# Attention stage: which tile splits a late piece of the input, and where the DMA queue waits for all splits

## The reference

```
qkv = x @ w_qkv.T                       # 16 heads of 32
q, k = [q*cos, q*sin], [k*cos, k*sin]   # angle = theta * position
per chunk of 128 tokens:
  scores = (q @ k.T) * diag_decay
  o      = scores @ v + (q*q_decay) @ state
  state  = block_decay*state + (k*k_decay).T @ v
x = layernorm(x + o @ w_proj.T)
```

## Time and profile before

| | |
|---|---|
| median of 3 runs | 1555.37 us (1551.93 to 1556.06) |
| the profiled execution | 1554.85 us |
| its span, first to last instruction | 1553.0 us |
| PE busy | 1402.9 us, 90% |
| DVE, POOL, ACT busy | 900.2, 763.5, 661.8 us |
| mean granted PE clock | 0.956 |
| attention stage | about 0 to 296 us of the span |

### The profile page before, as it was taken

How to read it: one execution, slowest core, us unless ns; L and a number is a source line. 1 busy time by engine, 2 the same in 40 slices (tenths; PEclk the granted TensorE clock), 3 DMA queues, 4 the chain that set the end, 5 groups by cost and what they waited for, 6 DMA issues and landing times.

```text
span 1553.0 us, 31650 instructions
## 1 busy us (share of the span) xinstructions
PE 1402.9 (90%) x10327; PEld 770.8 (50%) x10328; DVE 900.2 (58%) x1826; ACT 661.8 (43%) x1250; POOL 763.5 (49%) x691
## 2 busy tenths in 40 slices
PE   5999999799999999999886469999999999999990
PEld 2554555444444444445443226666666666666650
DVE  7765566677757576636988864444444444444435
ACT  7322222455444545423445434444444444444443
POOL 4555454510101101333645356766767677777755
PEclk9999999899999999999998579999999999999995
DMA  8776976698796969522312636888988998776866
GB/s 274 150 136 129 192 150 119 156 318 298 233 287 231 297 223 298 183 72 82 84 23 95 227 100 122 179 184 176 196 193 176 205 190 194 138 113 90 178 81 228
DMA packets 213453, 271.73 MB, mean 175 GB/s; under 512 B 133993, under 2 KB 135561, under 8 KB 212368
## 3 DMA queue, kind: packets, MB, share of 16 engines
q1 hardware_dynamic: 177776, 211.40, 46.8%
q0 software_dynamic: 35616, 59.58, 23.8%
HBM read 158.92 MB, written 101.71 MB: 168 GB/s over the span
## 4 chain that ended last, share of the span: by engine, by line
PE 77%; DVE 13%; DMA 3%; issue 2%; ACT 2%; POOL 2%; SPq 0%; DVEq 0%; ACTq 0%; POOLq 0%
PE bank L888 20%; PE bank L909 11%; PE bank L721 7%; PE bank L715 6%; PE bank L738 6%; PE bank L593 6%; PE bank L601 5%; PE bank L879 5%; PE bank L668 2%; DMA ARENA<-ARENA 2%; PE bank L898 2%; DVE ARENA L1253 1%; PE bank L632 1%; PE bank L633 1%; PE bank L660 1%
## 5 line engine op out<-in xcount | busy, mean ns | idle before, releaser
L888 PE MATMUL bank<-ARENA,XT 128*128 x1908 | 364.7, 327 | 2.1 <-issue 1.5
L1804 POOL DMA_INDIRECT accs<-X,WA x159 | 252.8, 1590 | 99.9 <-issue 39.4
L888 PEld LDWEIGHTS bank<-ARENA,XT 128*128 128x128 f16 x1908 | 180.5, 98 | 125.3 <-issue 9.4
L1343 DVE COPY XT<-bank 128x1024 f16<-128x1024 f16 x159 | 110.0, 692 | 186.0 <-PE bank L879 158.4
L1797 POOL DMA_INDIRECT XT<-x_rows,WA x159 | 166.6, 1048 | 86.9 <-issue 43.6
L909 PE MATMUL bank<-ARENA,XT 128*128 x795 | 197.4, 379 | 1.1 <-issue 1.0
L1382 ACT ACTIVATE ARENA<-ARENA 128x512 f16<-128x512 f32 (+2 forms) x128 | 89.3, 708 | 224.1 <-DVE ARENA L1101 132.0
L1622 ACT ACTIVATE XT<-bank 128x192 f32<-128x192 f32 x159 | 52.5, 330 | 287.8 <-PE bank L888 249.7
L593 PE MATMUL bank<-XT,STG 128*128 128x512 f16 x640 | 151.5, 384 | 7.4 <-DVE ARENA L1147 7.3
L1650 POOL TENSOR_TENSOR rstd<-mv,mhalf 128x1 f32<-128x1 f32 x28 | 5.7, 202 | 280.0 <-DVE mv L958 280.0
L601 PE MATMUL bank<-WA,XT 128*128 128x512 f16 x540 | 124.7, 380 | 1.9 <-DVE ARENA L1044 1.9
(11 more groups left out here) (244 smaller groups left out, 2173.6 us busy)
## 6 DMA issues: line engine op xcount, KB each, us to landing
w_scratch<-WA SPq DMA_DIRECT2D x64, 640.0 KB, 3.9
ARENA<-w_scratch SPq DMA_DIRECT2D x64, 640.0 KB
ARENA<-w_exp SPq DMA_DIRECT2D x48, 640.0 KB, 5.3
WA<-w_exp SPq DMA_DIRECT2D x16, 640.0 KB, 5.1
ARENA<-ARENA SPq DMA_DIRECT2D x32, 256.0 KB, 4.1
accs<-ARENA SPq DMA_DIRECT2D x20, 256.0 KB, 3.2
X<-x SPq DMA_DIRECT2D x4, 1024.0 KB, 5.6
ARENA<-wc SPq DMA_DIRECT2D x8, 512.0 KB, 6.1
```

The lines of the kernel that those rows point to most:

```text
L888: mm = pe.matmul(d, xTb[k.u % 2][:, a * KD + kd, :], weights(sl, b, kd * 2 * DFF, 2 * DFF), start=(a, b, kd) == (0, 0, 0), stop=(a, b, kd) ...
L1343: dve.tensor_copy(xTb[k.u % 2].rearrange("p c n -> p (c n)"), bank[k.u % 2][:, :].bitcast(F16)).then_inc(xt_sb, 1)
L1804: pool.indirect_dma_start(accs, bass.IndirectOffsetOnAxis(blkout[:, i:i + 1], 0), yD[i % 8], None, compute_op=ALU.add).then_inc(y_out[i % ...
```

## The change

Which late piece is handled in which tile is now a table: pieces 10 and 11 in tile 1, 12 in tile 2, none in tile 3, 13 to 15 in tiles 4 to 6 as before. PE's wait for all eight splits goes from before tile 7 to before tile 11, with a wait for six before tile 7, and its loop of tiles 7 to 14 becomes two. SP's wait for all eight splits goes from behind load_x(2) and load_x(3) to ahead of each of the int8 loads, that is from after turn(7) to after turn(9).

```diff
         LATE = 10
+        late = {1: (10, 11), 2: (12,), 4: (13,), 5: (14,), 6: (15,)}
...
                 elif n < 9:
                     load_x(n - 5)
+                elif n < 12:
                     sp.wait_ge(x_split, len(x_pieces))
-                elif n < 12:
                     sp.dma_start(*raws[n - 9]).then_inc(b_raw, 16)
...
             with pe.Fori(TB - 1, 2 * TB - 1) as t:
                 attention(t, False, False)
+            pe.wait_ge(x_split, 6)
+            with pe.Fori(2 * TB - 1, 3 * TB - 1) as t:
+                attention(t, False, False)
             pe.wait_ge(x_split, len(x_pieces))
-            with pe.Fori(2 * TB - 1, NT - 1) as t:
+            with pe.Fori(3 * TB - 1, NT - 1) as t:
                 attention(t, False, False)
...
-                if isinstance(t, int) and 1 <= t <= NPA - LATE:
-                    hi_piece(LATE + t - 1)
+                if isinstance(t, int):
+                    for n in late.get(t, ()):
+                        hi_piece(n)
...
-                if isinstance(t, int) and 1 <= t <= NPA - LATE:
-                    split_piece(LATE + t - 1)
+                if isinstance(t, int):
+                    for n in late.get(t, ()):
+                        split_piece(n)
```

## The result

The changed kernel takes 1543.56 us (median of 4 runs, 1542.99 to 1544.77) against 1555.7 for the kernel before beside it: a ratio of 0.9929, interval 0.9915 to 0.9944. The forecast was 1544.0.

A forecast was written before the change was run, and what follows sets the result against it. PE, busy 1402.9 us or 90% of the span, was taken as the bound. Terms -4.70 - 9.16 + 1.81 + 1.2 = -10.85 us took 1554.85 to 1544.0 us; range 1539.0 to 1550.0.

The forecast's parts named there:

- The gap before tile 7: First layer's attention: with both waits moved, PE's idling before tile 7 and its scores goes, clock stays up: -9.16 us.
- Rival 2: Tile 7: the load of a quarter of x delays the transposes, scores still wait; 6.7 us won, 1548.1; chance 0.15.
- The second hold in tile 1: POOL's second split holds DVE's third angle step, lengthening PE's gap before L1044 to 3.1 us: +1.81 us, bounds 0 to 3.6.
- The gap before tile 3: With piece 11 split in tile 1, PE's wait before tile 3 and the slower matmuls behind it go: -4.70 us.
- The loop cut in two: PE's loop of tiles 7 to 14: one more entry into fresh code shows nothing uncovered: 0, at most some tenths.
- The sum: Whole kernel: -4.70 - 9.16 + 1.81 + 1.2 = -10.85 us, from 1554.85 to 1544.0.
- the clock (1.2): Tile 2: PE's clock falls around the 3.1 us gap, slowing matmuls: +1.2 us, bounds 0 and 1.7.
- Rival 1: Tile 1: the second split is free, DVE's third angle step goes ahead of POOL, gap stays 1.31; 1541.0 us; chance 0.15.
- Rival 3: Across the kernel: most is given back by fresh loop code, clock falls elsewhere and the port; about 1552 us; chance 0.07.
- Rival 4: Tiles 1 and 2: ACT waits for piece 11 or 12 not yet landed, PE stops too; slower; chance 0.03.

## Why the prediction was right, point by point

- **The gap before tile 7, -9.16.** Measured -9.16 (31.30 against 40.46), with both waits gone, no long wait of SP for POOL and no idle PE before the scores. Rival 2, with the 1 MB load, falls: the q transpose of tile 7, issued 5.5 us behind the load, took 4.2 us and the k transpose 6.3. The prediction took both waits away together and did not say which one costs more; putting each back alone shows it (SP's +9.9, PE's +5.3 in tiles 7 and 8).
- **The second hold in tile 1, +1.81.** Measured +1.82, with two steps of 2.51 and 2.52 us and the gap of PE at 3.12 (3.1 said). None, one, two and three splits gave 0, 1, 2 and 3 held DVE instructions, so the exclusion is shown.
- **The gap before tile 3, -4.70.** Measured -4.06. No wait of L669 for POOL is left, but tile 3 is 16.29: PE waits 0.47 us for the k transpose, which takes 7.68 us instead of 6.18, and that is most of the 0.64 us by which the tile is long. This was missed. I had compared the start of the transposes with PE's arrival only at their usual 6.18.
- **The loop cut in two, 0.** Missed, with small and opposite pieces: +0.21 in tile 11, -1.47 in the last tile. The row I rested it on (the start of out_proj in the last tile) shows that PE does not wait for its code; it does not show what fetching the code does to the transposes.
- **The sum, -10.85.** The next layer begins exactly 10.85 us earlier. That it agrees to the last digit is luck: tile 3, tile 5, tile 1 and the first mark lose 2.4 us against the sum, tile 11 and the way to the next layer 0.3, and the clock (1.2) and the last tile (1.5) give it back.
- **Rival 1** (13.9 us less) was wrong for the change, but describes the kernel with one split in each tile: 12.9 us less by its ratio. **Rival 3** wanted 6.2 us or more given back; tiles 1, 3, 5 and 11, the first mark and the way to the next layer gave back 2.7. **Rival 4**: no wait of ACT's L1383 for a load is in the trace.

Two things stay open. Tile 1 is 16.4 to 16.7 us in all eleven edited kernels' profiles and 15.87 in that of before. In two of them (the changed kernel's and that with one split in each tile) the first mark stands at 38.83 us and half clock reaches 2.2 to 2.4 us into the tile, and PE is busy 0.8 to 0.9 us longer by it (16.49 and 16.59 us against 15.68), the whole difference; in the nine others the mark stands at 37.1 to 37.7 and PE waits 0.87 to 1.10 us for ACT before out_proj. Why the first mark moves was not tried. And the two measurements of the changed kernel, -11.0 and -7.2 us by their ratios, differ by more than the stretches of the attention stage do; I can only say that the part behind it scatters that much.

## What to carry to other kernels

When two engines wait for the same event, look for the one whose queue holds transfers that others need: here that wait cost 9.9 us and the other 5.3, and moving the other alone gained nothing. A helper's work that is pulled forward into a quiet engine can still stop its neighbour, so ask what the other engine runs in those microseconds, and place it where that engine reads PSUM or idles; here both pieces in tile 0 instead of tile 1 were worth a further 3.3 us in tile 2. (The whole stage is 4.3 us shorter, 242.33 against 246.62, but the rest is small differences that this edit was not meant to make, such as the long transpose of tile 5, which comes and goes.) Write a clock loss behind a gap of this length down as two cases, not as one number.

## What the hardware showed that I had not expected

**Instruction fetches go with stretched DMA transposes.** The instruction queue q8 moves packets of some 16 KB over the same DMA engines. From tile 3 on, the twelve profiles hold 29 transposes that took 5.9 to 6.1 us instead of 4.2 (q) or 7.4 to 7.7 instead of 6.2 (k), and in each of the 29 a q8 packet was under way. Not each packet makes one: several fell beside a transpose that kept its time, and several beside one of 4.4 to 5.2 us. In the changed kernel (two places of the chain of waits, and the instruction queue's row from 86 to 87 us):

```profile
81.07 7.68 DMA ARENA<-ARENA
...
107.34 5.88 DMA ARENA<-ARENA
```

```profile
q8 instruction: 1, 0.02, 7.4%
```

A long transpose costs 0.2 to 0.8 us where PE has work to run beside it (tiles 3 to 6 and 11) and 1.3 to 1.9 us where it has none (last tile: 17.59 and 17.63 us with a long k transpose, 15.7 to 16.3 without). In tile 3, at the entry to a new loop, it comes in every profile without a gap there; the one in tile 5 comes in tile 4, 5, 6 or 7 or not at all. That the packet is the cause is argued from this coincidence; adding loops added packets and one long transpose, which supports it but does not prove it.

**The same length of gap can cost the clock or not.** Idle for 3.11 to 3.12 us, three of six profiles kept 2.4 GHz. In the three others the clock fell 0.6 us before PE's gap ended, 0.04 us behind its end, or 0.9 us behind it. With 3.50 and 3.74 us in tiles 3 and 7 each of the five such gaps lost 1.3 to 1.7 us, and with 1.30 us none lost anything. But 3.50 us is no border either: before the first matmul of the feed-forward layer PE idles 3.4 to 3.8 us in each of the twelve profiles, and in two of them (the waits alone, the pieces alone) the clock stays at 2.4 GHz. PE's timeline there, first of the changed kernel, then of the one with the waits alone:

```profile
285.45 2.29 PE L719 MATMUL bank<-XT,WA 128*128 128x512 f16 x8 [3.78 <-issue]
287.54 3.21 PE L725 MATMUL bank<-XT,ARENA 128*128 128x512 f16 x8
```

```profile
286.26 1.89 PE L719 MATMUL bank<-XT,WA 128*128 128x512 f16 x8 [3.78 <-issue]
287.98 1.89 PE L725 MATMUL bank<-XT,ARENA 128*128 128x512 f16 x8
```

The gap is 3.78 us in both; the sixteen matmuls behind it take 5.3 us in one and 3.6 in the other. So in this range the length of the gap does not decide alone. What does was not tried.
